# Decay attention: LayerNorms as whole-group sums, squares and products, and the value products of four heads over four column strips

## Chip, core and metric

The kernel runs on one core of one Trainium2 chip, in one launch. The metric is the device time in microseconds; the kernel before takes 3803.72 us, the median of 3 runs (3796.95 to 3818.18). Engines are named as in the profile: PE is TensorE (PEld its weight loads), DVE VectorE, ACT ScalarE, POOL GpSimd.

## What is computed

The reference is a small tower over 64 sequences of tokens with width 64: an embedding with gates, an attention layer, a block with attention and eight experts, a "decay attention" with a convolution in front, and a selected MLP. The change lies in the decay attention alone, which is (x is the LayerNorm of the residual h, eps 1e-5; D = 64, 8 heads of width 8, K = 5 taps):

```python
low  = conv1d_causal(x, conv_w) + conv_b
hid  = _layernorm(low + sqrt_beta ** 2 * (x - low) + x, ln_w, ln_b)      # eps 1e-12
q, k, v = proj(q_w, q_b), proj(k_w, k_b), proj(v_w, v_b)
scores = q @ k.T / sqrt(dk)
p_ = softmax(where(mask, scores, -1e32)) * mask
dist = sqrt(clip((p_.sum(-1) - cumsum(p_)) * |i - j|, 0))
scores = where(mask, scores * clip(exp(dist * gamma), 1e-5, 1e5), -1e32)
p = softmax(scores); p[..., 0, :] = 0
h = h + (p @ v) @ out_w.T + out_b
```

A sequence has 128 positions in this kernel's layout, so a score matrix of one head and one sequence is 128 x 128.

## The kernel before

`phase_decay_attention` treats four sequences as a group (GB = 4, W = 512 columns) and one head of a group as a unit. There are 32 groups of 8 heads, so 256 units. Every engine runs the same loop over steps k (16 to a turn of a hardware loop, two groups), and each engine's program for a step is written out by hand: its order is the order in which the statements stand in `body`. Engines meet at semaphores (`Signals`; `now(n)` waits for item n of the counter, `before(n)` for item n-1, `past(q)` for the item 4 earlier, `ago(q, k)` for the one k earlier).

In step k the units in flight are: unit k is scored (PE L1582 to L1588) and its first softmax begun (DVE L1902, L1911; ACT L1752); unit k-1 is scanned (DVE L1887) and scaled (POOL L1470, L1474); unit k-2 goes through logarithm and two exponentials (ACT L1731, L1738, L1747); unit k-3 is weighed and its maximum taken (DVE L1898, L1906) and shifted (POOL L1479); unit k-4 gets its second exponential (ACT L1735); unit k-5 is transposed (PE L1601) and copied out of PSUM (ACT L1743, `pT`); unit k-6 is multiplied with its values (PE L1615). Four units share one PSUM bank `bO`, each in a strip of 32 partitions; in step k with (k-7) % 4 = 3 the bank is copied (ACT L1725) and transposed back (PE L1628), one step later DVE normalises it (L1874, L1880). A score bank `bS[u]` is free for unit k when unit k-4 has been weighed.

Before the scores of a unit PE issues some bf16 products into the same bank whose result is overwritten (`AGAIN`, 4, 6, 6, 3, 3, 3, 3 and 6 of them for the eight heads; "dummies" in the prediction).

Beside the units, `beside` runs the stages around the attention, at step j = k % 8 of group n: `norm` for group n+3 (LayerNorm 1: DVE at j = 3 and 5, ACT at 4), `filter` for group n+2 (transpose at j = 2, convolution at 3 to 6, statistics of LayerNorm 2 at 7), `project` for group n+1 (DVE makes `hn` at j = 0, PE transposes it at 1, q, k and v follow at 3 to 7), `finish` for group n-2 (output product and residual, j = 0 to 2). Three passes of `norm`, `filter` and `project` alone run ahead of the loop.

The convolution is five accumulated f32 products for each sequence; its weights `conv` are prepared once by DVE, ahead of the loop (`link` chains these instructions). The value products of one unit before:

```python
r = slice(h % QUAD * STRIP, (h % QUAD + 1) * STRIP)
for b in range(GB):
    last = nc.tensor.matmul(bO[r, b * P:(b + 1) * P], v[s][:, b, h, :],
                            pT[u][:, b * P:(b + 1) * P], start=True, stop=True)
last.then_inc(S["attended"], 1)
```

Of the kernel before, what the change touches and what calls it, by code (L numbers as in the profile page):

```python
# [6 lines left out]
ALU = mybir.AluOpType  # L7
# [1296 lines left out]
def phase_decay_attention(nc, dram, H, ident, NB):  # L1304
# [15 lines left out]
    with ExitStack() as ctx:  # L1320
# [20 lines left out]
        st, mv, rstd = m.sb("d_st", [P, GB, 6]), m.sb("d_mv", [P, GB, 2]), m.sb("d_rstd", [P, GB])  # L1341
        st2, mv2, rstd2 = m.sb("d_st2", [P, GB, 6]), m.sb("d_mv2", [P, GB, 2]), m.sb("d_rstd2", [P, GB])
# [11 lines left out]
        def slots(name, shape):  # L1354
# [4 lines left out]
        p2, pT = slots("d_p2", [P, W]), slots("d_pT", [P, W])  # L1359
# [19 lines left out]
                    scalar="log_var rstd_made xT_kept log_var2 rstd2_made hT_kept q_kept*2 k_kept*2 v_kept yT_kept",  # L1379
                    vector="stats moments centred stats2 moments2 centred2 h_made", gpsimd="hTr_kept")  # L1380
# [55 lines left out]
        with nc.Block() as block:  # L1436
# [8 lines left out]
            def _(pool):  # L1445
# [41 lines left out]
            def _(pe):  # L1487
# [10 lines left out]
                class Work(Beside):  # L1498
                    def filter(self, n, j):
                        if j == 2:  # L1500
                            pe.wait_ge(G["centred"], G.now(n))
# [17 lines left out]
                    def project(self, n, s, j):  # L1519
                        if j == 1:  # L1520
                            pe.wait_ge(G["centred2"], G.now(n))
# [46 lines left out]
                def body(i, k, lo, hi):  # L1568
# [35 lines left out]
                    if on:  # L1604
                        j = k - LAG_PV
# [29 lines left out]
            def _(act):  # L1635
# [50 lines left out]
                class Rates(Beside):  # L1686

                    def norm(self, n, j):
                        if j == 4:
                            act.wait_ge(G["moments"], G.now(n))  # L1690
                            act.wait_ge(G["centred"], G.before(n))
                            nc.scalar.activation(rstd[:], mv[:, :, 1], ACT.Ln, bias=1e-5).then_inc(G["log_var"], 1)
# [3 lines left out]
                    def filter(self, n, j):  # L1696
                        if j == 7:
                            act.wait_ge(G["moments2"], G.now(n))
                            act.wait_ge(G["centred2"], G.before(n))
                            nc.scalar.activation(rstd2[:], mv2[:, :, 1], ACT.Ln, bias=1e-12).then_inc(G["log_var2"], 1)  # L1700
# [3 lines left out]
                class Both(Beside):  # L1704

                    def norm(self, n, j):
                        rates.norm(n, j)
# [8 lines left out]
                def body(i, k, lo, hi):  # L1716
# [42 lines left out]
            def _(dve):  # L1759
# [22 lines left out]
                link(nc.vector.tensor_tensor(conv[0:D, TAPS - 1, :], conv[0:D, TAPS - 1, :], diag[:], ALU.add))  # L1782
                dve.wait_ge(fold, 1)
# [26 lines left out]
                class Work(Beside):  # L1810
                    def norm(self, n, j):
                        if j == 3:
                            dve.wait_ge(G["centred"], G.before(n))
                            for b in range(GB):
                                last = nc.vector.bn_stats(
                                    st[:, b, :], H[:, bass.ds(n * GB + b, 1), :].rearrange("p b d -> p (b d)"))
                            last.then_inc(G["stats"], 1)
                            dve.wait_ge(G["stats"], G.now(n))
                            dve.sem_inc(passed, 1)
                            for b in range(GB):  # L1820
                                last = nc.vector.bn_aggr(mv[:, b, :], st[:, b, :])
                            last.then_inc(G["moments"], 1)
                        if j == 5:
                            dve.wait_ge(G["rstd_made"], G.now(n))
                            dve.wait_ge(G["x_turned"], G.before(n))
                            for b in range(GB):
                                last = nc.vector.tensor_scalar(
                                    xn[:, b, :], H[:, bass.ds(n * GB + b, 1), :].rearrange("p b d -> p (b d)"),
                                    mv[:, b, 0:1], rstd[:, b:b + 1], ALU.subtract, ALU.mult)
                            last.then_inc(G["centred"], 1)  # L1830

                    def filter(self, n, j):
                        if j == 7:
                            dve.wait_ge(G["filtered"], G.now(n))
# [494 lines left out]
```

## Time and profile before

| | |
|---|---|
| median of 3 runs | 3803.72 us |
| lowest, highest | 3796.95, 3818.18 us |
| profiled execution, its time | 3843.11 us |
| its span, first to last instruction | 3841.3 us |
| mean granted TensorE clock of the span | 0.922 |
| PE busy | 3600.5 us (94%) |
| DVE busy | 2351.2 us (61%) |
| ACT busy | 1807.6 us (47%) |
| POOL busy | 1340.4 us (35%) |
| first and last score product (L1588) | 2200.9, 3610.1 us |

The span is one execution, some 40 us above the median of the timed runs. Busy times are unions of instruction durations. PE's matmuls overlap in their printed durations, so what one costs is read from the distance of starts. The phase of the change lies between about 2,160 and 3,640 us of the span. A row of a group of instructions reads: line, engine, operation, output and inputs, shapes, count, then busy time and mean duration in ns, then the idle time in front of them and what ended it.

### The profile page before, as it was taken

How to read it: one execution, taken by the hardware profiler on the slowest of the kernel's cores; microseconds unless marked ns; L12 is line 12 of the kernel's file. 1: busy time of each engine (PE TensorE's matmuls, PEld its weight loads, DVE VectorE, ACT ScalarE, POOL GpSimd, SP SyncE). 2: the span in 40 equal slices, each digit the busy share in tenths (PEclk: the TensorE clock that was granted, in tenths of full speed). 3: DMA queues.
4: the chain of work that ended last, by engine and by line, in shares of the span. 5: the costliest groups of instructions: out<-in, count | busy, mean ns of one | idle time of the engine just before them, and what ended most of it. 6: DMA issues, size and time to landing. Idle time of an engine off the chain costs nothing. (4 is left out here: it accounts for less than half of the span.)

```text
span 3841.3 us, 64998 instructions
## 1 busy us (share of the span) xinstructions
PE 3600.5 (94%) x21447; PEld 2492.5 (65%) x21558; DVE 2351.2 (61%) x5341; ACT 1807.6 (47%) x3601; POOL 1340.4 (35%) x1395
## 2 busy tenths in 40 slices
PE   7996999999976999999999799999999999999766
PEld 6885676666653555555555467777777777777555
DVE  4694454444446544454445378888888878888643
ACT  2342333333332233233323167777777777777642
POOL 5460121111121000000000056666666666666461
PEclk9996798878787999999999689999999999999876
DMA  1110000000000000000000000000000000000002
GB/s 39 28 40 5 1 0 0 0 0 0 0 20 1 1 0 0 0 0 0 0 0 0 10 1 1 0 0 0 0 0 0 0 0 0 0 0 0 3 1 44
DMA packets 29609, 18.70 MB, mean 5 GB/s; under 512 B 23562, under 2 KB 26891, under 8 KB 29540
## 3 DMA queue, kind: packets, MB, share of 16 engines
q0 software_dynamic: 6144, 9.84, 1.1%
q1 hardware_dynamic: 23396, 7.99, 0.9%
q8 instruction: 37, 0.61, 0.1%
q14 instruction: 32, 0.26, 0.0%
HBM read 13.63 MB, written 4.19 MB: 5 GB/s over the span
## 5 line engine op out<-in xcount | busy, mean ns | idle before, releaser
L1285 DVE TENSOR_TENSOR prod<-c_h,act 128x512 f32<-128x512 f32 x352 | 243.5, 692 | 480.5 <-PE c_h L1137 396.5
L1217 ACT ACTIVATE act<-c_h 128x512 f32<-128x512 f32 x352 | 210.2, 597 | 655.8 <-PE c_h L1137 655.8
L1470 POOL TENSOR_TENSOR d_decay<-d_later,d_pos 128x512 f32<-128x512 f32 x256 | 326.1, 1274 | 478.8 <-DVE d_later L1887 478.8
L1164 PEld LDWEIGHTS c_out<-e_w,hid 128*128 128x128 f32 x2816 | 340.6, 191 | 79.5 <-issue 79.3
L1164 PE MATMUL c_out<-e_w,hid 128*128 128x64 f32 x2816 | 388.7, 281 | 0.1
L1887 DVE TENSOR_TENSOR_SCAN d_later<-d_cont,d_ex 128x512 f32<-128x512 f32 x256 | 314.2, 1228 | 49.7 <-ACT d_ex L1752 46.2
L1588 PEld LDWEIGHTS d_S<-d_kT,d_qT 8*128 8x128 f32 x2048 | 249.9, 188 | 110.9 <-issue 110.9
L1111 POOL TENSOR_TENSOR x_rest<-flatT,x_hm 64x512 f32<-64x512 bf16 (+1 forms) x33 | 38.2, 1157 | 748.8 <-ACT x_hm L1197 724.8
L1588 PE MATMUL d_S<-d_kT,d_qT 8*128 8x128 f32 x2048 | 299.1, 285 | 0.0
L1479 POOL TENSOR_TENSOR d_p<-d_p,d_mx 128x512 f32<-128x512 f32 x256 | 266.0, 1039 | 60.3 <-DVE d_mx L1906 59.0
L1582 PE MATMUL d_S<-d_hide,d_ident_b 128*128 128x512 bf16 x1088 | 283.1, 385 | 0.0
L991 DVE TENSOR_REDUCE b_mx<-b_S 128x4 f32<-128x512 f32 x128 | 88.6, 692 | 314.8 <-PE b_S L749 314.8
L1474 POOL TENSOR_TENSOR d_decay<-d_decay,d_rtot 128x512 f32<-128x512 f32 x256 | 266.1, 1039 | 36.7
L1615 PE MATMUL d_O<-d_pT,d_v 128*32 128x128 f32 x2048 | 273.3, 277 | 0.4 <-ACT d_attT L1725 0.4
L1137 PE MATMUL c_h<-x_hm,e_w_mm 128*128 128x512 bf16 x688 | 261.5, 380 | 3.8 <-ACT wT L1210 1.3
L1137 PE MATMUL c_h<-x_hl,e_w_lh 128*128 128x512 bf16 x658 | 249.9, 380 | 0.8
L1137 PE MATMUL c_h<-x_hm,e_w_hh 128*128 128x512 bf16 x655 | 248.7, 380 | 0.0
L1902 DVE TENSOR_REDUCE d_mx<-d_S 128x4 f32<-128x512 f32 x256 | 176.4, 689 | 113.1 <-PE d_S L1588 112.6
L1292 DVE TENSOR_TENSOR hid<-c_wb,prod 128x512 f32<-128x512 f32 x352 | 239.6, 681 | 0.1
L1615 PEld LDWEIGHTS d_O<-d_pT,d_v 128*32 128x32 f32 x2048 | 203.8, 110 | 44.2 <-issue 43.1
L1743 ACT ACTIVATE d_pT<-d_T 128x512 f32<-128x512 f32 x256 | 152.7, 596 | 152.0 <-PE d_T L1601 150.2
L1514 PE MATMUL d_X<-d_conv,d_xT 64*128 64x64 f32 (+1 forms) x1360 | 210.4, 293 | 1.5 <-ACT d_xT L1656 1.4
(320 smaller groups left out, 7412.6 us busy)
## 6 DMA issues: line engine op xcount, KB each, us to landing
out_h<-g_Y SPq DMA_DIRECT2D x8, 512.0 KB, 4.0
rows<-in_table,idx POOLq DMA_INDIRECT x128
e_w<-in_e_w SPq DMA_DIRECT2D x2, 704.0 KB
e_w<-in_e_w SPq DMA_DIRECT2D x1, 352.0 KB
d_pos<-in_d_pos SPq DMA_DIRECT2D x1, 256.0 KB
d_cont<-in_d_cont SPq DMA_DIRECT2D x1, 256.0 KB
g_w<-in_g_w SPq DMA_DIRECT2D x3, 64.0 KB, 2.1
d_win<-in_d_win SPq DMA_DIRECT2D x1, 146.2 KB
```

The lines of the kernel that those rows point to most:

```text
L1137: last = nc.tensor.matmul(out[:], w[:, cols], x[:], start=(j == 0), stop=(j == 2))
L1164: last = nc.tensor.matmul(bo[:, b * D:(b + 1) * D], hid[u][:, b * P:(b + 1) * P], w2[:, c, :], start=(c == 0 and b == 0), stop=(c == NCH - ...
L1285: nc.vector.tensor_tensor(prod[u][:], b3[u][:], act1[u][:], ALU.mult).then_inc(S["multiplied"], 1)
L1292: nc.vector.tensor_tensor(hid[v][:], bw[v][:], prod[v][:], ALU.mult).then_inc(S["weighted"], 1)
L1470: pool.tensor_tensor(decay[u][:], later[u][:, 0:W], pos[:], ALU.mult).then_inc(S["placed"], 1)
L1474: pool.tensor_tensor(grouped(decay[u][:], P), grouped(decay[u][:], P), over(rtot[u][:], P), ALU.mult).then_inc(S["scaled"], 1)
L1479: pool.tensor_tensor(grouped(p2[u][:], P), grouped(p2[u][:], P), over(mx2[u][:], P), ALU.subtract).then_inc(S["shifted2"], 1)
L1514: last = nc.tensor.matmul(bX1[:, b * D:(b + 1) * D], xT[0:rows, b, tap:tap + P], conv[0:rows, tap, :], start=(tap == 0), stop=(tap == TAPS ...
L1582: nc.tensor.matmul(bS[u][:], ident_b[:], hide[:, None, :].to_broadcast([P, GB, P]), start=True, stop=True)
L1588: last = nc.tensor.matmul(bS[u][:, cols], qT[s][r, c, cols], kT[s][r, c, cols], start=False, stop=(b == GB - 1))
L1615: last = nc.tensor.matmul(bO[r, b * P:(b + 1) * P], v[s][:, b, h, :], pT[u][:, b * P:(b + 1) * P], start=True, stop=True)
L1887: nc.vector.tensor_tensor_scan(later[u1][:, 1:1 + W], cont[:], ex[u1][:], 0.0, ALU.mult, ALU.add).then_inc(S["scanned"], 1)
```

## The change

1. LayerNorm 1 (`norm`): bn_stats, bn_aggr and one tensor_scalar for each sequence on DVE go. In their place DVE sums the group (`mean`, j = 0), POOL scales the sums and subtracts the means (`hc`, j = 1), ACT squares (`sq`, j = 3), DVE sums the squares (`ss`, j = 3), ACT makes `rstd` (j = 4, now with scale 1/D), POOL multiplies (`xn`, j = 5).
2. LayerNorm 2 (`filter`, `project`): the mean of each row is taken out of the convolution's weights once, in the set-up (two more DVE instructions), so that the output is centred already. ACT squares it out of PSUM (`sq2`, j = 7), DVE sums the squares (j = 7), ACT makes `rstd2`, DVE multiplies the group in one instruction (`hn`, j = 0).
3. Value products: units k-9 to k-6 together, in the step with (k-6) % 4 = 3, in the order of sequences outside and heads inside, so that consecutive products write different strips. `pT` has 8 buffers in place of 4, and ACT's copy waits for `attended` of the unit 8 earlier in place of 4.

```diff
-        p2, pT = slots("d_p2", [P, W]), slots("d_pT", [P, W])
+        p2, pT = slots("d_p2", [P, W]), [m.sb(f"d_pT{u}", [P, W]) for u in range(2 * SLOTS)]
...
+                    def norm(self, n, j):
+                        if j == 1:
+                            pool.wait_ge(G["summed"], G.now(n))
+                            pool.wait_ge(G["scaled"], G.before(n))
+                            pool.sem_inc(passed, 1)
+                            pool.tensor_scalar(mean[:], mean[:], 1.0 / D, None, ALU.mult).then_inc(G["mean_made"], 1)
+                            pool.wait_ge(G["mean_made"], G.now(n))
+                            pool.sem_inc(passed, 1)
+                            pool.tensor_tensor(hc[:], H[:, bass.ds(n * GB, GB), :], over(mean[:], D), ALU.subtract)\
+                                .then_inc(G["centred"], 1)
+                        if j == 5:
+                            pool.wait_ge(G["rstd_made"], G.now(n))
+                            pool.wait_ge(G["x_turned"], G.before(n))
+                            pool.sem_inc(passed, 1)
+                            pool.tensor_tensor(xn[:], hc[:], over(rstd[:], D), ALU.mult).then_inc(G["scaled"], 1)
...
                     on, q, u = unit(LAG_PV)
-                    if on:
-                        j = k - LAG_PV
+                    if on and (k - LAG_PV) % QUAD == QUAD - 1:
+                        j = k - LAG_PV - (QUAD - 1)
                         s, h = (j // GQ) % 2, j % GQ
                         if h == 0:
                             pe.wait_ge(G["v_kept"], G.now(group_of(i, k, LAG_PV)))
-                        if h % QUAD == 0:
-
-                            pe.wait_ge(Q["attT_kept"], Q.before(quad_of(i, k + QUAD - 1, LAG_PV)))
+
+                        pe.wait_ge(Q["attT_kept"], Q.before(quad_of(i, k, LAG_PV)))
                         pe.wait_ge(S["pT_kept"], S.now(q))
-                        r = slice(h % QUAD * STRIP, (h % QUAD + 1) * STRIP)
                         for b in range(GB):
-                            last = nc.tensor.matmul(bO[r, b * P:(b + 1) * P], v[s][:, b, h, :],
-                                                    pT[u][:, b * P:(b + 1) * P], start=True, stop=True)
-                        last.then_inc(S["attended"], 1)
+                            for e in range(QUAD):
+                                last = nc.tensor.matmul(bO[e * STRIP:(e + 1) * STRIP, b * P:(b + 1) * P],
+                                                        v[s][:, b, h + e, :],
+                                                        pT[(j + e) % (2 * SLOTS)][:, b * P:(b + 1) * P],
+                                                        start=True, stop=True)
+                        last.then_inc(S["attended"], QUAD)
...
+                    def norm(self, n, j):
+                        if j == 3:
+                            act.wait_ge(G["centred"], G.now(n))
+                            act.wait_ge(G["spread"], G.before(n))
+                            nc.scalar.activation(sq[:], hc[:], ACT.Square).then_inc(G["squared"], 1)
+
                     def filter(self, n, j):
+                        if j == 7:
+                            act.wait_ge(G["filtered"], G.now(n))
+                            act.wait_ge(G["spread2"], G.before(n))
+                            nc.scalar.activation(sq2[:], grouped(bX1[:, 0:GB * D], D), ACT.Square)\
+                                .then_inc(G["squared2"], 1)
...
-                        act.wait_ge(S["attended"], S.past(q2))
-                        nc.scalar.activation(pT[u2][:], bT[:], ACT.Copy).then_inc(S["pT_kept"], 1)
+                        if not (isinstance(q2, int) and q2 < 2 * SLOTS):
+                            act.wait_ge(S["attended"], S.ago(q2, 2 * SLOTS))
+                        nc.scalar.activation(pT[(k - LAG_TURN) % (2 * SLOTS)][:], bT[:], ACT.Copy)\
+                            .then_inc(S["pT_kept"], 1)
...
+                link(nc.vector.tensor_reduce(tapsum[:], conv[:], AX, ALU.add))
+                link(nc.vector.scalar_tensor_tensor(conv[:], over(tapsum[:], D), -1.0 / D, conv[:], ALU.mult, ALU.add))
...
                     def norm(self, n, j):
+                        if j == 0:
+                            dve.wait_ge(G["centred"], G.before(n))
+                            nc.vector.tensor_reduce(mean[:], H[:, bass.ds(n * GB, GB), :], AX, ALU.add)\
+                                .then_inc(G["summed"], 1)
                         if j == 3:
...
+                            dve.wait_ge(G["squared"], G.now(n))
+                            dve.wait_ge(G["rstd_made"], G.before(n))
+                            nc.vector.tensor_reduce(ss[:], sq[:], AX, ALU.add).then_inc(G["spread"], 1)
-                        if j == 5:
...
 
                     def filter(self, n, j):
                         if j == 7:
...
+                            dve.wait_ge(G["squared2"], G.now(n))
+                            dve.wait_ge(G["rstd2_made"], G.before(n))
+                            nc.vector.tensor_reduce(ss2[:], sq2[:], AX, ALU.add).then_inc(G["spread2"], 1)
 
                     def project(self, n, s, j):
                         if j == 0:
                             dve.wait_ge(G["rstd2_made"], G.now(n))
                             dve.wait_ge(G["h_turned"], G.before(n))
...
+                            nc.vector.tensor_tensor(hn[:], grouped(bX1[:, 0:GB * D], D), over(rstd2[:], D), ALU.mult)\
+                                .then_inc(G["scaled2"], 1)
```

## Rows read from the trace of the kernel before

**Rows 1.** The page: busy time of PE, and the span in 40 equal slices.
```profile
PE 3600.5 (94%) x21447; PEld 2492.5 (65%) x21558; DVE 2351.2 (61%) x5341; ACT 1807.6 (47%) x3601; POOL 1340.4 (35%) x1395
PE   7996999999976999999999799999999999999766
PEclk9996798878787999999999689999999999999876
```

**Rows 2.** Windows: a group, its shortest (k=0) and longest (k=6) step.
```profile
core 0: us, PE busy (x) PEld busy (x) DVE busy (x) ACT busy (x) POOL busy (x), PEclk, DMA share, GB/s
2703.34:2747.30 43.96, 43.96 (x288) 31.05 (x286) 36.11 (x77) 32.86 (x63) 27.08 (x26) 1.00 0.00 0
...
2720.85:2727.13 6.28, 6.28 (x42) 4.52 (x40) 3.22 (x6) 4.23 (x8) 3.35 (x3) 1.00 0.00 0
...
2732.34:2736.63 4.29, 4.29 (x31) 3.01 (x31) 3.85 (x10) 3.58 (x9) 2.37 (x3) 1.00 0.00 0
```

**Rows 3.** Timeline of PE, one step (k=2): start, duration, count.
```profile
2742.20 1.46 PE L1582 MATMUL d_S<-d_hide,d_ident_b 128*128 128x512 bf16 x6
...
2743.81 1.15 PE L1588 MATMUL d_S<-d_kT,d_qT 8*128 8x128 f32 x8
2744.89 0.66 PE L1601 MATMUL d_T<-ident,d_p 128*128 128x128 f32 x4
2745.48 1.06 PE L1615 MATMUL d_O<-d_pT,d_v 128*32 128x128 f32 x8
2746.47 0.63 PE L1505 MATMUL d_X<-ident,d_xn 128*64 128x128 f32 x4
2746.93 0.60 PE L1628 MATMUL d_T<-ident,d_attT 128*128 128x128 f32 x4
2747.37 0.59 PE L1582 MATMUL d_S<-d_hide,d_ident_b 128*128 128x512 bf16 x2
```

**Rows 4.** Timeline of PE, the end of a step with a filter (k=3).
```profile
2706.96 1.47 PE L1514 MATMUL d_X<-d_conv,d_xT 64*128 64x64 f32 x10
2708.26 1.08 PE L1534 MATMUL d_X<-d_hT,d_win 65*128 65x512 f32 x2
2709.18 0.81 PE L1582 MATMUL d_S<-d_hide,d_ident_b 128*128 128x512 bf16 x3
```

**Rows 5.** Last phase: timeline of PE, and L2038 within 20 ns (3701.48:3701.50).
```profile
3701.49 1.13 PE L2038 MATMUL g_H<-g_xT,g_w 64*128 64x256 f32 x8
3702.55 0.66 PE L2048 MATMUL g_B<-g_w,g_hid 128*128 128x64 f32 x4
...
L2038 PE MATMUL g_H<-g_xT,g_w x2: 480/480/480, 3701.5 to 3701.5; 64*128 64x256 f32 x2
```

**Rows 6.** Timeline of DVE, one step with nothing beside; idle time in brackets.
```profile
2740.01 0.68 DVE L1902 TENSOR_REDUCE d_mx<-d_S 128x4 f32<-128x512 f32 x1
...
2742.58 1.29 DVE L1887 TENSOR_TENSOR_SCAN d_later<-d_cont,d_ex 128x512 f32<-128x512 f32 x1 [0.70 <-ACT d_ex L1752]
...
2744.00 0.67 DVE L1898 SCALAR_TENSOR_TENSOR d_p<-d_decay,d_S 128x512 f32<-128x512 f32 x1
```

**Rows 7.** Groups of instructions of the whole span, shapes apart.
```profile
L1902 DVE TENSOR_REDUCE d_mx<-d_S 128x4 f32<-128x512 f32 x256 | 176.4, 689 | 113.1 <-PE d_S L1588 112.6
...
L1850 DVE TENSOR_SCALAR d_hn<-d_X,d_mv,d_rstd 128x64 f32<-128x64 f32 x132 | 36.0, 336 | 0.5 <-ACT d_rstd L1702 0.5
L1815 DVE BATCH_NORM_STATS2 d_st<-H 128x6 f32 x120 | 17.9, 212 | 0.0
...
L1821 DVE BATCH_NORM_AGGREGATE d_mv<-d_st 128x2 f32<-128x6 f32 x140 | 13.3, 158 | 5.4 <-DVE d_st L1815 4.7
L974 DVE TENSOR_REDUCE b_ss<-b_sq 128x4 f32<-128x256 f32 x32 | 12.4, 389 | 0.1
L649 POOL TENSOR_TENSOR b_fl<-b_x,b_ss 128x256 f32<-128x256 f32 x64 | 37.8, 612 | 155.8 <-ACT b_ss L861 155.8
L1677 ACT ACTIVATE d_v<-d_X 128x256 f32<-128x256 f32 x33 | 12.4, 375 | 4.8 <-issue 2.8 <-PE d_X L1545 2.1
```

More of the change, by code:

```diff
@@ L1500, in filter @@
                         if j == 2:
-                            pe.wait_ge(G["centred"], G.now(n))
+                            pe.wait_ge(G["scaled"], G.now(n))
                             pe.wait_ge(G["hT_kept"], G.before(n))
@@ L1520, in project @@
                         if j == 1:
-                            pe.wait_ge(G["centred2"], G.now(n))
+                            pe.wait_ge(G["scaled2"], G.now(n))
                             pe.sem_inc(passed, 1)
@@ L1689, in norm @@
                         if j == 4:
-                            act.wait_ge(G["moments"], G.now(n))
-                            act.wait_ge(G["centred"], G.before(n))
-                            nc.scalar.activation(rstd[:], mv[:, :, 1], ACT.Ln, bias=1e-5).then_inc(G["log_var"], 1)
+                            act.wait_ge(G["spread"], G.now(n))
+                            act.wait_ge(G["scaled"], G.before(n))
+                            nc.scalar.activation(rstd[:], ss[:], ACT.Ln, scale=1.0 / D, bias=1e-5).then_inc(G["log_var"], 1)
                             act.wait_ge(G["log_var"], G.now(n))
@@ L1697, in filter @@
                         if j == 7:
-                            act.wait_ge(G["moments2"], G.now(n))
-                            act.wait_ge(G["centred2"], G.before(n))
-                            nc.scalar.activation(rstd2[:], mv2[:, :, 1], ACT.Ln, bias=1e-12).then_inc(G["log_var2"], 1)
+                            act.wait_ge(G["spread2"], G.now(n))
+                            act.wait_ge(G["scaled2"], G.before(n))
+                            nc.scalar.activation(rstd2[:], ss2[:], ACT.Ln, scale=1.0 / D, bias=1e-12).then_inc(G["log_var2"], 1)
                             act.wait_ge(G["log_var2"], G.now(n))
@@ L1706, in norm @@
                     def norm(self, n, j):
+                        copies.norm(n, j)
                         rates.norm(n, j)
@@ L1817, in norm @@
[L1817 to L1822, printed above, removed]
-                        if j == 5:
[L1824 to L1830, printed above, removed]
+                            dve.wait_ge(G["squared"], G.now(n))
@@ L1832, in filter @@
+                            dve.wait_ge(G["rstd_made"], G.before(n))
+                            nc.vector.tensor_reduce(ss[:], sq[:], AX, ALU.add).then_inc(G["spread"], 1)
                     def filter(self, n, j):
                         if j == 7:
-                            dve.wait_ge(G["filtered"], G.now(n))
-                            dve.wait_ge(G["centred2"], G.before(n))
-                            for b in range(GB):
-                                last = nc.vector.bn_stats(st2[:, b, :], bX1[:, b * D:(b + 1) * D])
@@ L1838, in filter @@
-                            last.then_inc(G["stats2"], 1)
-                            dve.wait_ge(G["stats2"], G.now(n))
-                            dve.sem_inc(passed, 1)
-                            for b in range(GB):
-                                last = nc.vector.bn_aggr(mv2[:, b, :], st2[:, b, :])
-                            last.then_inc(G["moments2"], 1)
+                            dve.wait_ge(G["squared2"], G.now(n))
+                            dve.wait_ge(G["rstd2_made"], G.before(n))
@@ L1848, in project @@
                             dve.wait_ge(G["h_turned"], G.before(n))
-                            for b in range(GB):
-                                last = nc.vector.tensor_scalar(hn[:, b, :], bX1[:, b * D:(b + 1) * D], mv2[:, b, 0:1],
-                                                               rstd2[:, b:b + 1], ALU.subtract, ALU.mult)
-                            last.then_inc(G["centred2"], 1)
+                            nc.vector.tensor_tensor(hn[:], grouped(bX1[:, 0:GB * D], D), over(rstd2[:], D), ALU.mult)\
+                                .then_inc(G["scaled2"], 1)
                     def finish(self, n, s, j):
```

16 lines of the change are left out of this document (8 added, 8 removed).

## Prediction

> **What bounds the kernel now.** I read the page first. TensorE is busy 94% of the span, and the decay attention, which is slices 23 to 37, shows it at 9 in every slice with a granted clock at 9 (tenths) [rows 1]. Busy alone doesn't prove a bound, so I took the windows of one group of heads (8 units, the loop's natural period). It lasts 43.96 us and PE is busy for all of it; DVE is busy 36.1, ACT 32.9, POOL 27.1, at granted clock 1.00, the full 2.4 GHz [rows 2]. Then the timeline of PE itself: in a step each block starts when the one before has been issued, with no idle time and no releaser printed [rows 3]. The other engines are the ones that wait: DVE sits 112.6 us in the phase for the scores that PE makes [rows 7]. So one group costs what PE's instruction stream costs, 44 us, and 32 groups make about 1,409 of the 3,843 us. What takes work from DVE alone is worth nothing here; what shortens PE's stream is worth its full length, until DVE or ACT becomes the bound.
>
> **PE's stream, priced.** A start-to-start time is the true price, since the printed durations overlap. In one unit [rows 3]: a bf16 dummy of 512 columns 0.216 (seven such products, with one change of tile shape of 0.1, take 1.61), the eight score records 1.08 (2743.81 to 2744.89), the four transposes of p2 0.59, the eight records of the value products 0.99 (2745.48 to 2746.47), and the four transposes of xn 0.46. A value product is two records, so a record costs 0.124 on average. Four transposes cost 0.59 when value products (128x32 tiles) follow but 0.44 to 0.46 when only full-array work does (L1505 into L1628, L1628 into the dummies) [rows 3]. So going from one tile shape to another costs some 0.1 us: that is what makes 0.99 out of eight records of 0.109, together with 0.02 to 0.03 on the first spacing after it. The Trainium skill says the same of a change of tile shape ("TensorEngine Tiling (Array Packing)", Key Properties: changing the mode drains the engine, changing only the tile doesn't); the second half of that sentence no row here shows, and it separates two cases below.
>
> **Part 1, value products.** Now each unit issues its 4 (8 records) in one column strip. Afterwards three units of four issue none and the fourth issues 16 (32 records), b outside and strip inside, so neighbours lie in different strips.
>
> Removed: 6 blocks per group at 0.99 = 5.94 us. In the three steps where full-array work follows the transposes (k = 0, 2, 7) the detour through 128x32 vanishes too: 0.09 after the transposes and 0.02 to 0.05 behind it, 3 x 0.11 = 0.33. In the steps with filter matmuls (64-row tiles, L1514) a change of shape stays [rows 4]. Together 6.27 us per group.
>
> Added: 24 records in each of two bursts. Their price isn't in the trace, so it is bounded from both sides:
> - no overlap: 0.109 each, +2.62 per burst, +5.23 per group. Net gain 6.27 - 5.23 = 1.04 us.
> - full overlap: four strips run together, 8 rounds of 0.109, as long as one unit's block now; with about 0.1 for staggered starts, +0.2 per group. Net 6.1 us.
> - half: the two records of one product share a strip, so if the engine keeps strict order only the second record of one and the first of the next overlap: 16 x 0.116 in place of 0.87, +1.0 per burst. Net 4.3 us.
>
> Which row is nearest? The last phase has f32 products on two row strips (L2038). Two of its records start within 20 ns, and eight records of 256 columns take 1.06 us (3701.49 to 3702.55) [rows 5], where L1534 pays 0.92 for two of 512 columns, so 0.23 per 256 and 1.84 for eight [rows 4]. That is an overlap of 1.7, two strips fully together but for the entry. Tiles of the array do run side by side in f32, and the two records of one product don't stop it. Those are row strips; column strips need four different moving operands at once over all 128 rows, which no row shows. I take full overlap as likeliest. The Trainium skill supports it ("TensorE: Matmul & The Clock Gate", Measured speedup vs the span model: 2.38 with three column tiles at 512 columns); at that efficiency for four, an estimate, a burst takes 32 x 0.109 / 3.17 = 1.10 us and adds 0.23, a net of 5.8. The same page (Part 3, The mechanism) says that a weight load overlaps running matmuls only when the row group differs, and column strips share all four row groups. Here value-product loads already overlap matmuls of their own strip (the stream is gapless at 0.109 with a 0.11 load each), so I give that rule little weight; what it would give here is the no-overlap rival.
>
> **Part 2, LayerNorms.** DVE loses 8 bn_stats (0.21), 8 bn_aggr (0.16) and 8 tensor_scalar (0.34 for hn) per group: 5.7 us by means, some 4.5 of its stream because neighbours overlap. It gains three reduces (0.39) and one product of that size, 1.6 by means, about 1.4 of stream [rows 7]. Net -3 us of DVE per group. ACT gains two squares of 128x256 (0.375 as L1677), 0.75 us on 32.9 of 44. POOL gains two 128x256 products of 0.61 (L649) and a tiny scale (0.2), 1.4 us on 27.1 [rows 2, 7]. All lie beside PE: in the loop the normalised tile is wanted a group later (scaled at j=5, turned at j=2 of the next group), hn is made at step 0 and turned after step 1's burst. By itself this part is worth 0 while PE binds. If that cover is gone (PE's group below about 38.9 us) the DVE relief is worth up to 1.7 us per group. Outside the loop: two more DVE instructions in the set-up and longer hand-offs (DVE, POOL, ACT, DVE, ACT, POOL) in the three prologue passes, which nothing hides: +4 us in all.
>
> **What is next when PE gets shorter.** Full overlap gives PE 43.9 - 6.1 = 37.8 per group. DVE's chain from one score maximum to the next, with no wait on PE: three passes over 512 columns, then 0.70 idle for ACT's exponential, scan, reciprocal, weighing: 2740.01 to 2744.59 [rows 6], 4.6 us (the last start plus 0.59, the spacing of such operations). LayerNorm leftovers fit in the 0.70 hole. Eight of these plus 0.3 for y at one step: 37.1. So PE still binds by 0.7, but the steps are uneven. They run from 4.29 (k=0) to 6.28 (k=6) now [rows 2]; afterwards k=0 has 3.2, k=7 4.1, k=2 4.0, and the burst steps k=1 and k=5 keep 5.7 and 5.9. From the end of one unit's scores to the end of the next (dummies included, 0.216 each) PE then takes 5.9, 3.65, 3.6, 5.7, 3.4, 4.85 us from k=6 on, where DVE takes 4.6 each time (4.9 into k=3): it is 0, 0.95, 2.0, 0.9 and 2.45 us behind at k=7, 0, 1, 2 and 3. PE must not refill a score bank before DVE has weighed unit k-4, so the lag may be as long as what PE does behind its scores (the step less its dummies and 1.40 for the last bf16 product and the scores): 2.8 at k=3, 0.9 at k=0. It just fits; I allow 0.4 to 0.5 us of stalls per group, 38.3 in all, gain 5.6. ACT's cycle (3.4 of core work plus at most 1.0 of copies) is shorter than DVE's.
>
> **The sum.** 32 x 5.6 = 179, less 4 outside: 175 us. The profiled execution has 3,843.1 us; with the change 3,668. The median of the runs is 39 us below it; the loop ran at full clock already, so I take the same 175 from the median: 3803.7 - 175 = 3,629.
>
> **Rivals.**
> - Half overlap, strict order: 32 x 4.3 - 4 = 134, 3,670. For it: two records of a product want the same strip. Against it: rows 5's pairs. DVE never binds then.
> - No overlap (shared row groups or one moving stream): 32 x 1.04 - 4 = 29, 3,775. The gain is only changes of tile shape. The burst step grows to 8.5 us, the short ones fall to 3.2 to 5.3; PE stays gapless if DVE keeps up. For it: no row shows column strips together.
> - Slower: every change of strip costs what a change of shape does, about 0.12. A burst has 15 changes, +1.8 on top of no overlap, 3.6 per group; net 1.04 - 3.6 = -2.6, 32 x 2.6 + 4 = 87, so 3,891. It decides from 0.035 us per change on. Nothing in the trace shows adjacent records in different column strips, so only rows 5 (two row strips, 20 ns) speak against it.
> - Stalls eat the gain: overlap is full, but DVE or ACT can't follow uneven steps, 40.5 us per group instead of 38.3: 32 x 3.4 - 4 = 105, 3,699. If PE idles enough that its clock falls to 1.2 GHz, the range's upper end or worse; the idle bits expected are under 0.5 us in a step, and before the change the clock was 1.00 with none.
>
> **Chances.** Full overlap 0.45, half 0.17, stalls 0.13, no overlap 0.15, slower 0.10. 0.5% (19 us) is about what a measurement of this kernel can tell from no change. No overlap (29 us) could fall within it, and I give it a third of its weight, with a little from stalls: same 0.08, slower 0.10, faster 0.82. The likeliest case's own range is 3,605 (no DVE stall, 6.1 x 32) to 3,655. The stated range reaches over half overlap and stalls to no overlap: 3,600 to 3,780.
>
> **What would show it.** Right: 32 records of L1615 in about 1.1 us with starts a few ns apart, one such block in four units; a group of 38 to 38.5 us; DVE's waits for d_S small; clock 1.00. Half: the block 2 us, the group 39.7. None: 3.6 and 42.9. Slower: above 5 us. It is also wrong if PE shows idle time ended by DVE's weighing or ACT's pT copy, or if the LayerNorm's new waits hold POOL (in front of its decay products) or ACT's exponentials.

## The result and the profile after

The changed kernel takes 4,100.8 us (4 runs, 4,055.9 to 4,143.9) where the kernel before takes 3,806.7: ratio 1.073, 95% interval 1.063 to 1.084. It is 294 us slower; I had forecast 175 us less. Executions in a second, slower state are left out of every ratio here; where too few others remained, the table of experiments gives the two medians instead, and they say less.

The page of the profiled execution (4,115.8 us), its busy time and slices, against [rows 1]:

```profile
span 4113.9 us, 64559 instructions
PE 3841.2 (93%) x21447; PEld 2594.6 (63%) x21558; DVE 2294.6 (56%) x4656; ACT 1805.8 (44%) x3670; POOL 1441.4 (35%) x1500
...
PE   7996999999959999999979999999999999999857
...
PEclk9995979987879999999985678566766878666776
```

PE is as busy as before. What differs is the last line: in slices 25 to 37 the granted clock wanders between 5 and 8 tenths, where [rows 1] has 9 throughout. The score products now run from 2,191.8 to 3,882.0 us, 1,690 us in place of 1,409 (2,200.9 to 3,610.1). The 281 us lie in this phase.

Windows cut where the clock changes, with one whole group at full clock first, against [rows 2]:

```profile
core 0: us, PE busy (x) PEld busy (x) DVE busy (x) ACT busy (x) POOL busy (x), PEclk, DMA share, GB/s
2472.20:2511.20 39.00, 38.02 (x288) 26.30 (x287) 34.57 (x58) 32.25 (x65) 30.92 (x29) 1.00 0.00 0
2546.00:2563.00 17.00, 16.14 (x133) 11.39 (x132) 15.01 (x27) 12.80 (x26) 12.68 (x12) 1.00 0.00 0
2563.00:2604.00 41.00, 41.00 (x156) 26.48 (x155) 19.20 (x33) 19.97 (x39) 17.53 (x17) 0.50 0.00 0
2604.00:2621.00 17.00, 16.03 (x133) 11.21 (x130) 15.05 (x26) 12.80 (x27) 12.52 (x12) 1.00 0.00 0
```

The first row is the forecast come true: a group of 288 records takes 39.0 us, not 44.0. The other three are what half of the phase looks like: 17 us at 2.4 GHz with 133 matmuls, then 41 us at 1.2 GHz with 156, then 17 again. Such a group takes 58 us. Over 30 groups of the loop (by the distance of the starts of L1525, the first few left out) 14 are of this kind, 3 are at full clock throughout, at 39.03 us, and the others lie between 43.7 and 67.5; the mean of all is 53.07. Before, all 30 were at 1.00 and took 44.03. (53.07 - 44.03) x 32 = 289 us, within 5 us of the whole loss.

The timeline of PE, the end of step k = 1 and step k = 2 of one group, with the first rows of k = 3, against [rows 3]:

```profile
3002.95 1.08 PE L1634 MATMUL d_O<-d_pT,d_v 128*32 128x128 f32 x32
3003.96 0.63 PE L1544 MATMUL d_X<-ident,d_hn 128*64 128x128 f32 x4
...
3007.96 0.66 PE L1621 MATMUL d_T<-ident,d_p 128*128 128x128 f32 x4
3008.45 0.60 PE L1525 MATMUL d_X<-ident,d_xn 128*64 128x128 f32 x4
3009.84 0.79 PE L1649 MATMUL d_T<-ident,d_attT 128*128 128x128 f32 x4 [0.79 <-ACT d_pT L1777]
3010.41 1.49 PE L1602 MATMUL d_S<-d_hide,d_ident_b 128*128 128x512 bf16 x3
...
3012.26 2.07 PE L1608 MATMUL d_S<-d_kT,d_qT 8*128 8x128 f32 x8
```

Read from the top. Thirty-two value products take 1.01 us (3002.95 to 3003.96), where eight took 0.99 [rows 3]: the four strips run together in full. The transposes without value products behind them take 0.49 (3007.96 to 3008.45) in place of 0.59. Then comes something that was not there before: PE stands idle for 0.79 us until ACT has copied `pT`. And behind it everything is slow: the same eight score records print 2.07 us, 1.15 in [rows 3]. The group in which this happens runs at half clock until its step k = 7. Of the 35 stretches at half clock in this phase, 18 begin at this place; the others begin in steps k = 3 to 6, most of them in a projection (L1554, L1560).

That copy's own rows on ACT (same group) show why the wait exists:

```profile
3006.59 0.58 ACT L1758 ACTIVATE d_attT<-d_O 128x512 f32<-128x512 f32 x1
3007.07 0.58 ACT L1696 ACTIVATE d_hT<-d_X 64x512 f32<-64x512 f32 x1
3007.55 0.62 ACT L1764 ACTIVATE d_decay<-d_decay 128x512 f32<-128x512 f32 x1
3008.07 0.62 ACT L1768 ACTIVATE d_p<-d_p 128x512 f32<-128x512 f32 x1
3008.59 0.62 ACT L1771 ACTIVATE d_decay<-d_decay 128x512 f32<-128x512 f32 x1
3009.11 0.58 ACT L1777 ACTIVATE d_pT<-d_T 128x512 f32<-128x512 f32 x1
```

ACT is not idle for a moment; `pT` is the last of six instructions in a row. Before, in [rows 3], PE had 0.99 us of value products between the transposes into `bT` and the back transposes into the same bank, and they covered this.

### The profile page after: what moved, and what is told of

It reads as the page before. It is cut to its first block and busy times, and to the rows that moved or that the text cites. A ratio compares the mean times of both kernels' runs of the same rounds, so it can differ in the third digit from the quotient of the medians.

```text
span 4113.9 us, 64559 instructions
## 1 busy us (share of the span) xinstructions
PE 3841.2 (93%) x21447; PEld 2594.6 (63%) x21558; DVE 2294.6 (56%) x4656; ACT 1805.8 (44%) x3670; POOL 1441.4 (35%) x1500
## 5 line engine op out<-in xcount | busy, mean ns | idle before, releaser
L1608 PEld LDWEIGHTS d_S<-d_kT,d_qT 8*128 8x128 f32 x2048 | 325.4, 238 | 150.9 <-issue 150.9
L1904 DVE TENSOR_TENSOR_SCAN d_later<-d_cont,d_ex 128x512 f32<-128x512 f32 x256 | 347.0, 1356 | 111.3 <-ACT d_ex L1787 110.1
L1608 PE MATMUL d_S<-d_kT,d_qT 8*128 8x128 f32 x2048 | 384.1, 341 | 0.0
L1602 PE MATMUL d_S<-d_hide,d_ident_b 128*128 128x512 bf16 x1088 | 373.0, 480 | 4.4 <-DVE d_p L1915 3.4
L1534 PE MATMUL d_X<-d_conv,d_xT 64*128 64x64 f32 (+1 forms) x1360 | 299.0, 378 | 1.6 <-ACT d_xT L1688 1.6
L1534 PEld LDWEIGHTS d_X<-d_conv,d_xT 64*128 64x128 f32 (+1 forms) x1360 | 262.4, 276 | 57.9 <-issue 41.2
L1602 PEld LDWEIGHTS d_S<-d_hide,d_ident_b 128*128 128x128 bf16 x1088 | 128.7, 123 | 216.8 <-issue 159.3
```

What stands on the lines that cost most here:

```text
L1534: last = nc.tensor.matmul(bX1[:, b * D:(b + 1) * D], xT[0:rows, b, tap:tap + P], conv[0:rows, tap, :], start=(tap == 0), stop=(tap == TAPS ...
L1602: nc.tensor.matmul(bS[u][:], ident_b[:], hide[:, None, :].to_broadcast([P, GB, P]), start=True, stop=True)
L1608: last = nc.tensor.matmul(bS[u][:, cols], qT[s][r, c, cols], kT[s][r, c, cols], start=False, stop=(b == GB - 1))
L1904: nc.vector.tensor_tensor_scan(later[u1][:, 1:1 + W], cont[:], ex[u1][:], 0.0, ALU.mult, ALU.add).then_inc(S["scanned"], 1)
```

## The experiments

Each kernel was run beside the kernel before on the same chip; ratios are to that. "Groups at full clock" counts among 30 groups of the loop, as above; "mean" is over the 30. Both columns come from one profiled execution of each kernel. A kernel whose clock falls varies from run to run (one of them from 3,822 to 4,308 us), so small differences between such counts mean nothing.

| run | ratio (95% interval), or medians | groups at full clock, their length | mean of all |
|---|---|---|---|
| before | 1 | 30, 44.03 us | 44.03 |
| the change | 1.073 (1.063 to 1.084) | 3, 39.03 | 53.07 |
| products only | 1.076 (1.066 to 1.086) | 0 | 52.76 |
| norms only | 0.999 (0.994 to 1.003) | 30, 44.03 | 44.03 |
| one strip at a time | 1.025 (1.016 to 1.034) | 0 | 47.14 |
| wait filled | 0.999 (0.993 to 1.004) | 9, 38.99 | 43.72 |
| filled, 9 more at heads | 4,001.6 against 3,816.8 | 7, 40.86 | 48.64 |
| open, 9 more at heads | 1.032 (1.027 to 1.038) | 7, 40.91 | 46.32 |
| filled, 5 more at heads | 1.052 (1.047 to 1.057) | 3, 40.01 | 49.33 |
| filled, 34 spread out | 3,964.0 against 3,816.8 | 0 | 48.90 |
| filled, 2 moved to middle | 1.037 (1.024 to 1.049) | 7, 38.83 | 50.19 |
| filled, 2 added in middle | 1.003 (0.992 to 1.013) | 22, 40.08 | 43.69 |
| open, 2 added in middle | 3,952.4 against 3,863.3 | 15, 40.09 | 48.76 |
| filled, 4 added in middle | 0.981 (0.976 to 0.986) | 30, 41.39 | 41.39 |
| open, 4 added in middle | 1.015 (1.009 to 1.021) | 24, 41.41 | 44.21 |
| the same, filled, heads trimmed | 0.985 (0.981 to 0.990) | 30, 41.36 | 41.36 |
| filled, 4 in middle, old norms | 0.990 (0.986 to 0.993) | 29, 41.94 | 42.00 |
| filled, 3 added in middle | 0.980 (0.961 to 0.998) | 30, 40.75 | 40.75 |
| filled, 4 in middle, one strip at a time | 1.005 (0.999 to 1.011) | 30, 44.08 | 44.08 |

**Which half of the change?** Products only: the kernel before with the hunks of `pT`, of the value products and of ACT's copy. Norms only: the changed kernel with exactly these hunks taken back.

> The value products in bursts of 32 records over four column strips, LayerNorms as before. Clock theory (the clock falls because of what the bursts do to TensorE's stream): the clock alternates as with the whole change, a group takes 39 to 41 us at full clock and about 58 on average over the two levels, 4,050 to 4,150 us. Rival (the new LayerNorm steps on ACT and POOL delay the copies that TensorE waits for, and that wait brings the clock down): the clock stays at 1.00 and the kernel takes 3,640 to 3,700 us.

> The LayerNorms as whole-group sums, squares and products, the value products unit by unit as before. Clock theory: TensorE's stream is as before, the group stays at 44.0 us at clock 1.00, 3,800 to 3,815 us. Rival (the LayerNorm part is what costs): 3,900 or more, with the clock moving between its levels.

Measured 1.076 and 0.999. The products carry the whole loss, though with the old norms no group of the 30 is at full clock where the change has 3. With the norms alone the window of a group reads:

```profile
2671.50:2715.50 44.00, 44.00 (x287) 31.09 (x286) 34.11 (x58) 33.51 (x65) 29.29 (x29) 1.00 0.00 0
```

DVE is down by 2.0 us of busy time, ACT up by 0.7, POOL by 2.2 [rows 2], and the time stays: worth nothing while PE binds, as forecast.

**Overlap, or the order of the units? And the wait?** The first kernel exchanges the loops of the burst, the second fills the wait at k = 2. The expectation of the first counts 16 records to a strip; they are 8.

```diff
-                        for b in range(GB):
-                            for e in range(QUAD):
+                        for e in range(QUAD):
+                            for b in range(GB):
```
```diff
                         pe.wait_ge(Q["attT_kept"], Q.now(n))
+                        if k % GQ == 2:
+                            for _ in range(4):
+                                nc.tensor.matmul(bO[:], ident_b[:], hide[:, None, :].to_broadcast([P, GB, P]),
+                                                 start=True, stop=True)
```

> The changed kernel with the two loops of the burst exchanged: 16 records go to one strip, then 16 to... the next, so that only neighbours at the seams can overlap, with the wait of 0.8 us before the back transposes still there. If the wait alone brings the clock down: a burst of about 3.5 us, clock alternating, over 4,150 us. If the thinner stream (four records in the time of one) does it: clock 1.00, a group of about 43.7 us, 3,780 to 3,810 us.

> The changed kernel with four more bf16 products of 512 columns at k = 2, in the place of the wait of 0.8 us before the back transposes (0.86 us of work, written into the bank of the value products, which is free there and is overwritten later). If the wait brings the clock down: the clock stays at 1.00, a group takes 39.1 us, 3,640 to 3,660 us. If the stream as a whole is too thin: the clock still alternates, 3,900 to 4,100 us.

Neither theory survived whole. One strip at a time lies between its two numbers: the clock falls in every group, at k = 4 for 7 or 10 us instead of 41, mostly once more at k = 6 for 3 us, and never at k = 2. This kernel differs from the change in more than the burst, which the expectation did not foresee: its wait at k = 2 is half as long, 0.38 us on average over 1,200 us of the loop:

```profile
PE d_T L1649 <- ACT d_pT L1777: 9.5, 25, 0.4
```

Filling the wait won 290 us, but not the clock for good: of three groups about one keeps it, one loses it for 3 us at k = 6, and one loses it for 24 us, mostly at k = 4. Where, the timeline and the windows of the kernel with the wait filled show:

```profile
2434.84 0.38 PE L1604 MATMUL d_S<-d_hide,d_ident_b 128*128 128x512 bf16 x1
2435.15 1.15 PE L1608 MATMUL d_S<-d_kT,d_qT 8*128 8x128 f32 x8
2436.23 0.66 PE L1621 MATMUL d_T<-ident,d_p 128*128 128x128 f32 x4
2436.82 1.47 PE L1534 MATMUL d_X<-d_conv,d_xT 64*128 64x64 f32 x10
2438.12 1.72 PE L1560 MATMUL d_X<-d_hTr,d_win 65*128 65x512 f32 x2
...
2401.00:2438.30 37.30, 37.21 (x286) 26.27 (x286) 32.97 (x56) 31.52 (x64) 29.53 (x28) 1.00 0.00 0
2438.40:2462.20 23.80, 23.80 (x98) 14.62 (x97) 10.92 (x18) 12.24 (x24) 9.70 (x10) 0.50 0.00 0
```

No row has idle time in front of it. Scores on 8 rows of the array, transposes, a filter of 64-column products, a projection; in the middle of the projection (1.72 us for what takes 1.08) the clock drops. Before, each such step had 0.99 us of value products behind the transposes, as in [rows 3]. So two things had been taken away: cover for a wait at k = 2, and the value products in the middle of the filter steps.

**More work at the heads of the steps.** I tried to give it back in the cheapest place, by the numbers in `AGAIN`.

```diff
-    AGAIN = (4, 6, 6, 3, 3, 3, 3, 6)
+    AGAIN = (4, 6, 6, 6, 6, 4, 5, 6)      wait filled; and the same with the wait open
+    AGAIN = (4, 6, 6, 5, 5, 3, 4, 6)      wait filled
+    AGAIN = (4, 4, 4, 5, 5, 4, 4, 4)      wait filled
```

> The gap-filled kernel with nine more bf16 products per group, three more at k = 3 and k = 4, one at k = 5, two at k = 6 (AGAIN 4, 6, 6, 6, 6, 4, 5, 6): work put back into the steps from which the value products were taken. If the clock falls because those steps are too thin: clock 1.00, a group of 38.9 + 9 x 0.216 = 40.8 us, 3,690 to 3,715 us. If it falls for the way the four strips run together: it falls still, and the time is above 3,850 us.

> The same nine more products, but with the wait of 0.8 us at k = 2 left open. If a wait of that length is enough by itself to bring the clock down: falls at k = 2 in most groups, 3,850 to 4,000 us. If only the steps around it matter: clock 1.00, a group of 40.8 to 41 us, 3,690 to 3,720 us.

> Gap filled and five more products (two at k = 3 and 4, one at k = 6). If the thin steps are the cause and five are enough: clock 1.00, a group of 39.9 us, 3,665 to 3,685 us. If not enough: falls in some groups, 3,700 to 3,800 us.

> Gap filled, as many products as in the changed kernel (34 and the four of the gap), but spread 4, 4, 4, 5, 5, 4, 4, 4 in place of 4, 6, 6, 3, 3, 3, 3, 6. If it is the thinnest stretch that decides and not the total: the clock holds, a group of 38.9 us, 3,640 to 3,660 us. If the total decides: about as the gap-filled kernel, 3,780 to 3,850 us.

None of the four held the clock. Only the nine more products came out in ranges that were named: filled above 3,850 us, open between 3,850 and 4,000, though only 8 of the 61 falls of the open one are at k = 2 and not most. With the wait filled, five and nine more products made it worse than none, and most falls stood where they had stood, in the projection L1560 of k = 4 or 6: with five more, 27 of 28 at k = 4. With the wait open, nine more made it better (46.32 us per group where the change has 53.07), and this kernel was no slower than the one with the wait filled (runs of 3,898 to 3,951 and of 3,890 to 4,076 us). So filling the wait was not shown to help in every surrounding. More work at the heads of the steps did not bring the clock back; perhaps its place in the step counts.

**Work in the middle of the step.** The products go between the scores and the transposes, into the bank that the transposes write next:

```diff
+                        for _ in range(2 if k % GQ in (3, 4, 6) else 0):
+                            nc.tensor.matmul(bT[:], ident_b[:], hide[:, None, :].to_broadcast([P, GB, P]),
+                                             start=True, stop=True)
                         for b in range(GB):
                             cols = slice(b * P, (b + 1) * P)
                             last = nc.tensor.transpose(bT[:, cols], p2[u][:, cols], ident[:])
```

> The gap-filled kernel with two of the three bf16 products at the head of steps k = 3, 4 and 6 moved into the middle of the step, between the scores and the transposes (into the bank that the transposes write next). Nothing is added: 38.9 us per group at full clock. If the clock falls because the stretch from a step's scores over transposes, filter and projection to the next step's head has lost the value products in its middle: the clock holds at 1.00, 3,640 to 3,670 us. If the total of the work counts: as the gap-filled kernel or worse, 3,780 to 4,000 us.

> The same two products in the middle of steps k = 3, 4 and 6, but added to the three at the head: 6 x 0.216 = 1.3 us more per group, 40.2 us. If the missing middle is the cause and two products are enough: clock 1.00, 3,675 to 3,700 us, where nine and five more products at the head gave 4,002 and 4,006. If the way the four strips run together is the cause: above 3,850 us.

> As the one with products added in the middle, but the wait of 0.8 us at k = 2 is left open. If the wait is a cause of its own: the clock falls at k = 2 in part of the groups, 3,750 to 3,950 us. If only the middles count: clock 1.00, 3,675 to 3,710 us.

Moved from the head (`AGAIN` 4, 6, 6, 1, 1, 3, 1, 6) they didn't help: the heads of these steps could not be thinned for it. Added, they held the clock in 22 groups of 30, the most so far, at 40.08 us; the falls left were at k = 3, 4 and 6. That was not the 1.00 throughout that I had expected, and by its time alone (3,862 us beside 3,863 of the kernel before) this run could not refute the rival; the groups at full clock speak against it. With the wait open it was 15 of 30. Two products are 0.43 us; the value products had been 0.99. So four:

> The changed kernel, wait filled, with four bf16 products (0.86 us, nearly the 0.99 that the value products took there) in the middle of steps k = 3, 4 and 6. If the lost middles are the cause: the clock is at 1.00 in every group, 38.9 + 12 x 0.216 = 41.5 us per group, 2.5 us less than before, 80 us less in all, ratio 0.979. If the clock answers to the overlapped bursts: it falls still, ratio 1.00 or more.

> As the one with four products in the middle, but with the wait of 0.8 us at k = 2 open. If the wait is a cause of its own: falls at k = 2 or 3 in some groups, ratio 1.00 to 1.04. If only the middles count: clock 1.00, ratio 0.98.

> Four products in the middle of steps 3, 4 and 6, wait filled, and five fewer at the heads of steps 1, 2 and 7 (AGAIN 4, 4, 4, 3, 3, 3, 3, 5): 40.4 us per group. If the other steps have products to spare: clock 1.00, ratio 0.97. If not: falls at k = 0 to 2 or 7, ratio 0.99 to 1.05.

> Four products in the middle, wait filled, with the LayerNorms as before the change. The LayerNorm part takes 3 us of stream from VectorE, which is the bound only below about 38.9 us per group: with 41.5 us of TensorE work it is worth nothing here, the ratio is the same 0.98 as with the new LayerNorms. If VectorE stalls TensorE in uneven steps: a group of 42 to 42.5 us and falls of the clock at the waits, ratio 0.99 to 1.03.

Windows of a group and of 1,200 us with four in the middle and the wait filled, then a step k = 3 or 4 of it:

```profile
2518.40:2559.80 41.40, 41.21 (x305) 27.87 (x303) 34.68 (x58) 32.82 (x65) 30.98 (x29) 1.00 0.00 0
2300.00:3500.00 1200.00, 1195.91 (x8761) 808.94 (x8758) 1003.69 (x1654) 951.02 (x1857) 899.00 (x813) 1.00 0.00 0
...
2526.77 1.15 PE L1608 MATMUL d_S<-d_kT,d_qT 8*128 8x128 f32 x8
2527.85 1.04 PE L1620 MATMUL d_T<-d_hide,d_ident_b 128*128 128x512 bf16 x4
2528.73 0.60 PE L1624 MATMUL d_T<-ident,d_p 128*128 128x128 f32 x4
2529.26 1.47 PE L1534 MATMUL d_X<-d_conv,d_xT 64*128 64x64 f32 x10
```

Clock 1.00 in every group, 41.39 us each (expected 41.5), ratio 0.981 (expected 0.979). Its score products run from 2,210.6 to 3,538.8 us, 81 us less than before. This version beats both kernels. And the place of the products counts, not only their number: three in the middle of each of the steps 3, 4 and 6 (the last pair below) held the clock in 30 groups of 30, the same nine at the heads of steps 3 to 6 in 7, with the wait filled in both; the fastest runs took 3,706 and 3,890 us.

The same with the wait open, windows of a group that went well and of a fall, and the timeline at that fall:

```profile
2340.80:2382.20 41.40, 40.53 (x300) 27.53 (x299) 34.53 (x58) 32.76 (x65) 31.03 (x29) 1.00 0.00 0
2428.40:2476.20 47.80, 47.80 (x172) 28.86 (x171) 20.46 (x35) 20.12 (x39) 18.74 (x18) 0.50 0.00 0
...
2426.91 0.60 PE L1525 MATMUL d_X<-ident,d_xn 128*64 128x128 f32 x4
2428.29 0.96 PE L1652 MATMUL d_T<-ident,d_attT 128*128 128x128 f32 x4 [0.78 <-ACT d_pT L1780]
2429.04 1.06 PE L1602 MATMUL d_S<-d_hide,d_ident_b 128*128 128x512 bf16 x2
```

The only difference to the kernel above is that these 0.78 us are idle instead of filled. A group is no longer or shorter for it (41.41), yet 6 of 30 groups lose the clock, every time within this step, and the kernel is 1.5% slower than before instead of 1.9% faster. That here the wait is a cause of its own is shown. It is not enough each time: 24 groups pass it at full clock. Nor was filling it seen to help everywhere, as the pair with nine more at the heads shows.

Heads trimmed by five products: the clock held, but the group stayed at 41.36 where I expected 40.4. The waits of PE over 1,000 us, and below them those of the kernel with the old norms:

```profile
PE d_T L1656 <- ACT d_pT L1784: 12.8, 24, 0.5
PE d_S L1602 <- DVE d_p L1922: 8.3, 24, 0.4
...
PE d_S L1582 <- DVE d_p L1908: 12.3, 24, 0.7
```

In the trimmed kernel PE stands 0.53 us per group for ACT's copy and 0.35 for DVE's weighing: the products taken away had been in the place of waits. Those two waits, 0.5 and 0.4 us long, left the clock alone. With the old norms PE waits 0.5 us per group for DVE (up to 0.7; behind one wait of 0.68 us the clock fell for 3 us), and a group takes 41.94 instead of 41.39: 32 x 0.55 = 18 us are what the LayerNorm half is worth once PE's stream is short. I had expected nothing at 41.5; the rival that I had put beside it, a group of 42 to 42.5 us, came closer.

**The edge, and the overlap at full clock.**

> The wait filled and three bf16 products in the middle of steps 3, 4 and 6, where two left falls of the clock in some groups and four in none. If three are enough: 40.7 us per group, clock 1.00, ratio 0.975. If not: falls in a few groups, ratio 0.98 to 1.01.

> As the one with four products in the middle, but the burst goes through one strip after the other (eight records each), so that only the seams can overlap. If the overlap is what shortens the stream: bursts of about 3.5 us in place of 1.0, 41.4 + 5.0 = 46.4 us per group, 160 us above the same kernel with overlap, ratio 1.02. If the order of units alone did it: ratio 0.98.

Three products are enough: 30 of 30 groups at full clock, 40.75 us, the shortest that held; its ratio, 0.980, isn't told apart from that of four. One strip at a time, same filling, gives 44.08 us per group and ratio 1.005. So the overlap of the strips is worth 2.7 us per group, 86 us; the new order of units without it only pays for its filling of 16 products. But I expected 46.4. The burst itself:

```profile
2780.12 0.66 PE L1624 MATMUL d_T<-ident,d_p 128*128 128x128 f32 x4
2780.70 2.46 PE L1637 MATMUL d_O<-d_pT,d_v 128*32 128x128 f32 x32
2783.09 1.47 PE L1534 MATMUL d_X<-d_conv,d_xT 64*128 64x64 f32 x10
```

2.39 us for 32 records in four runs of eight, 22 times 0.109 and not 32 times.

## Why the prediction was wrong

**The step that failed** is the price of a group. "What is next when PE gets shorter" ends at 38.3 us, and the sum takes 32 groups at that length, because "the loop ran at full clock already". A lower clock stood in the sum at nothing. The stall rival named a fall to 1.2 GHz, put no price on it and set it aside because "the idle bits expected are under 0.5 us in a step". In its place the runs showed a wait of 0.79 us at k = 2, and falls of the clock in filter steps with no wait at all: 53.07 us per group where the same kernel takes 39.03 at full clock. These 14.0 us, 449 in 32 groups, stand against 160 us gained.

**What was missed.** I asked who fills PE's time, not what the value products covered. I priced the six blocks taken out at 0.99 us each and did not follow the rows behind them: L1601 writes `bT`, ACT copies it, L1628 writes `bT` again, and in step k = 2 the blocks between were L1615 and L1505 [rows 3]. With L1615 gone, the transposes of L1525 alone stand between them, and the back transposes start 1.39 us after these do (3008.45 to 3009.84). I looked for the next wait in DVE's chain only, though the signs of being wrong did name idle time ended by ACT's `pT` copy.

**A misread row.** The second loss had left a trace in the kernel before. The prediction says that slices 23 to 37 show 9 for PE and for the clock. [rows 1] prints 7 and 6 for slice 23, and a clock of 8 for slice 24; only from slice 25 on do both stay at 9. In slice 24 lies the loop's first group, in which no unit has come to its value products yet (the first L1615 starts at 2236.4):

```profile
2218.95 1.15 PE L1588 MATMUL d_S<-d_kT,d_qT 8*128 8x128 f32 x8
2220.03 1.47 PE L1514 MATMUL d_X<-d_conv,d_xT 64*128 64x64 f32 x10
2221.33 1.26 PE L1540 MATMUL d_X<-d_hTr,d_win 65*128 65x512 f32 x2
2222.39 1.49 PE L1582 MATMUL d_S<-d_hide,d_ident_b 128*128 128x512 bf16 x3
...
2222.20:2246.00 23.80, 23.80 (x74) 14.25 (x74) 12.96 (x22) 11.08 (x22) 11.40 (x11) 0.50 0.00 0
```

It is step k = 4: scores, filter, projection, no idle time printed, and in the projection the clock drops for 24 us, as it did later in the kernel with the wait filled. That a busy PE need not keep the clock stood in other phases too: from 900 to 1,000 us PE is busy for 100.00 of 100 us at a granted clock of 0.78. These rows give no price for the loop, but they would have given the clock a term.

**Right, by its own steps.** The bound: with DVE relieved alone nothing changed (0.999). Full overlap of the strips: 32 records in 1.01 us, where I had put about 1.1. PE's stream: 37.8 forecast, 38.02 busy per group at full clock. The group at full clock: 38.3 forecast with 0.4 to 0.5 of stalls, 39.03 measured with 0.97 (0.78 on ACT, 0.19 on DVE). The size 5.6 us per group would have been 5.0: 160 us, had the clock stayed. Of smaller terms, the LayerNorms took 2.0 us per group from DVE where I had about 3 (norms only), and gave POOL 2.2 where I had 1.4; neither is on the path. In the likeliest case's own range, 3,605 should read 3,612 (6.1 x 32, less 4).

**The slower rival** had the right sign and the wrong mechanism: the burst took 1.01 us, where no overlap plus 0.12 per change of strip would have been above 5. That the whole came out slower is not its merit.

**What stays open.** Two causes are shown by filling each: the wait (1.015 against 0.981, with the middles filled) and the missing middles (with the wait filled, from 9 groups of 30 at full clock to 22 with two products and 30 with three or four). Why more work at the heads of the same steps made the falls more frequent (3 and 7 groups of 30 at full clock, against 9), why the open wait did no visible harm there, and why a fall lasts 10 us in one kernel and 41 in another is not settled. Nor is the part of the burst's own density. The change and its order of one strip at a time differ in it, and the falls are longer with the overlap, but they differ in the length of the wait too. Once the middles and the wait were filled, both held at 1.00.

## What to carry to other kernels

When PE is the bound, a matmul can have two jobs that its price doesn't show, and here it had both: it covered the way of a PSUM bank through another engine's copy, and it kept the clock. Before taking blocks out of a stream that runs at granted clock 1.00, list for each place what is left between a write to a bank and the next write to it, and look at the stretch of thin products (few rows, few columns, transposes) that grows together there. If a shorter stream comes out slower, read the granted clock by windows first, then fill each thinned place by itself: here 16 small products (0.216 us each) turned a loss of 7% into a gain of 2%.

## What the runs showed of the hardware

- Four f32 products on four column strips, each with its own moving operand of 128 rows, run together in full: 32 records in 1.01 us, 8 on one strip in 0.99. The two records of one product are no obstacle. Here the trace doesn't bear out the rule of the Trainium skill ("TensorE: Matmul & The Clock Gate", Part 3, The mechanism) that weight loads overlap running matmuls only across row groups: all four strips share their row groups.
- Even in an order of eight records to one strip, then eight to the next, 32 records took 2.39 us in place of 3.5. Part of the records of neighbouring strips must have run together.
- At 1.2 GHz a stretch of 41 us holds 156 matmuls, at 2.4 GHz one of 17 us holds 133. Where the clock came back depends on the kernel: in the change 24 of 35 such stretches ended at the head of step k = 7, with one strip at a time 31 of 54 ended in step k = 5, in its burst or the filter behind it.
- With PE never waiting for more than 0.2 us the clock still fell, in steps with 8-row scores, 64-column filters and transposes. A wait of 0.78 us brought it down in 6 groups of 30 with four products in the middles. At waits of 0.4 us (one strip at a time) and 0.5 us (filled, 34 spread out; heads trimmed) in the same place it fell in none of some 30 groups each.
